# Window maxima stacked in 128 rows, zero products in TensorE's waits, and a rearranged expert tail

## The reference

```
h = rmsnorm(layernorm(x)); q, k, v = h@Wq, h@Wk, h@Wv          # 16 heads of 8
q_phi, k_phi = taylor(q@Wqf), taylor(k@Wkf)                    # 1, x, x_i*x_j
lin = causal linear attention of q_phi, k_phi, v in chunks of 128 tokens,
      with a state (kv, ksum) that is carried from chunk to chunk
win = softmax(where(allowed, q@k.T / sqrt(8), -inf)) @ v       # allowed: the last 64 tokens
x = x + layernorm(x) + concat(lin, win) @ Wout
y = layernorm(x)
topv, topi = top_k(y@Wgate + bgate, 2); topw = softmax(topv)   # 2 of 8 experts
z = (y@W1[e] + b1[e]) * (y@W2[e] + b2[e])
o = silu(z@Wg[e] + bg[e]) * (z@Wl[e] + bl[e])
out = x + sum over the 2 experts of topw * (o@W3[e] + b3[e])
```

## Time and profile before

| | |
|---|---|
| median of 3 runs | 412.84 us (408.07 to 413.14) |
| the profiled execution | 410.21 us, span 408.3 us |
| busy of the span | PE 84%, PEld 73%, DVE 62%, ACT 52%, POOL 54% |
| mean granted TensorE clock | 0.946 of full speed |
| chain that ended last | PE 73%, SPq 9%, DMA 6%, DVE 4%, ACT 2% |

### The profile page before, as it was taken

The page is one execution under the profiler, slowest core; times in us unless marked ns, Lnnn a source line. Parts: engine busy times, 40 slices in busy tenths (PEclk is TensorE's granted clock), DMA queues, the critical chain, the costliest instruction groups (busy, mean ns, idle before and its releaser), DMA issues.

```text
span 408.3 us, 15626 instructions
## 1 busy us (share of the span) xinstructions
PE 343.6 (84%) x5603; PEld 298.1 (73%) x5603; DVE 251.6 (62%) x1001; ACT 211.6 (52%) x574; POOL 219.0 (54%) x368
## 2 busy tenths in 40 slices
PE   0768795699999999999999941699999999999920
PEld 0345584588878788888888830599999999999910
DVE  4665553268986688888887747255555555555515
ACT  0465563366565766676667620355555555555410
POOL 5363554155666577767765554012666655666510
PEclk9999999699999999999999985599999999999985
DMA  7746886878887877554342000223333333333028
GB/s 197 196 123 115 141 218 149 99 166 180 182 188 177 170 134 133 135 128 92 80 92 63 18 32 28 73 60 120 118 122 125 120 127 134 114 119 119 18 67 244
DMA packets 91966, 50.20 MB, mean 123 GB/s; under 512 B 56874, under 2 KB 86220, under 8 KB 91890
## 3 DMA queue, kind: packets, MB, share of 16 engines
q1 hardware_dynamic: 88898, 44.48, 46.0%
q0 software_dynamic: 2272, 4.46, 3.4%
q10 hardware_dynamic: 720, 0.26, 0.3%
HBM read 29.52 MB, written 11.98 MB: 102 GB/s over the span
## 4 chain that ended last, share of the span: by engine, by line
PE 73%; SPq 9%; DMA 6%; DVE 4%; issue 4%; ACT 2%; POOL 1%; DVEq 0%; POOLq 0%; ACTq 0%
PE ps L748 8%; PE ps L754 8%; PE ps L642 6%; PE ps L589 5%; PE ps L720 5%; PE ps L723 4%; PE ps L731 4%; PE ps L638 4%; PE ps L688 4%; PE ps L681 4%; PE ps L601 3%; PE ps L608 3%; SPq L382 3%; SPq L368 3%; PE ps L664 2%
## 5 line engine op out<-in xcount | busy, mean ns | idle before, releaser
L1300 POOL TENSOR_SCALAR_AFFINE_SELECT amat<-amat 128x512 f32<-128x512 f32 x64 | 41.0, 641 | 66.4 <-ACT amat L820 65.7
L1334 POOL DMA_INDIRECT results<-qas,mrowid x39 | 38.2, 979 | 68.1 <-ACT qas L887 68.1
L1103 DVE TENSOR_REDUCE mrow<-ps 128x4 f32<-128x512 f32 x64 | 43.8, 685 | 36.5 <-PE ps L589 36.4
L833 ACT ACTIVATE pmat<-ps 128x512 f32<-128x512 f32 x64 | 38.4, 600 | 54.0 <-PE ps L642 54.0
L1172 DVE SCALAR_TENSOR_TENSOR qas<-ps,bcol,qas 128x128 f32<-128x128 f32 x78 | 26.5, 351 | 34.3 <-ACT qas L893 30.8
L875 ACT ACTIVATE qas<-ps,bcol 128x128 f32<-128x128 f32 x78 | 24.4, 364 | 38.4 <-PE ps L720 38.4
L1182 DVE SCALAR_TENSOR_TENSOR qas<-ps,bcol,qas 128x128 f32<-128x128 f32 x78 | 23.9, 347 | 29.0 <-ACT qas L875 21.7
L820 ACT ACTIVATE amat<-ps 128x512 f32<-128x512 f32 x64 | 38.5, 602 | 1.9 <-PE ps L601 1.7
L1261 POOL DMA_INDIRECT routed<-routed_row,slot x32 | 32.6, 1018 | 12.9 <-issue 5.8
L642 PE MATMUL ps<-minus_ident,mrow 128*128 128x128 bf16 x256 | 36.0, 221 | 0.0
L642 PE MATMUL ps<-minus_ident,mlow 128*128 128x128 bf16 x256 | 35.7, 220 | 0.0
(11 more groups left out here) (170 smaller groups left out, 913.8 us busy)
## 6 DMA issues: line engine op xcount, KB each, us to landing
kv_tok<-w SPq DMA_DIRECT2D x31, 256.0 KB
qa_parts<-wgl SPq DMA_DIRECT2D x12, 256.0 KB, 3.3
ks<-k_parts SPq DMA_DIRECT2D x32, 96.0 KB
qas<-qa_parts SPq DMA_DIRECT2D x32, 96.0 KB
xin<-routed SPq DMA_DIRECT2D x39, 72.0 KB, 1.9
ks<-k_parts SPq DMA_DIRECT2D x32, 64.0 KB
qas<-qa_parts SPq DMA_DIRECT2D x32, 64.0 KB
w<-in_W SPq DMA_DIRECT2D x2, 1024.0 KB
```

What stands on the lines that cost most here:

```text
L833: a_(pmat[:, u % 2].rearrange("p g t -> p (g t)"), ps[:, ST, :], ACT.Exp).then_inc(exp_done, 1)
L1103: v.tensor_reduce(mrow[:, b], ps[:, SQ, :].rearrange("p (a k) -> p a k", k=CH), AX.X, ALU.max).then_inc(max_done, 1)
L1300: q.affine_select(out=amat[:, u % 2], in_=amat[:, u % 2], compare_op=ALU.is_ge, fill=0.0, base=0, pattern=[[0, 4], [1, CH]], channel_multi ...
L1334: q.indirect_dma_start(results, bass.IndirectOffsetOnAxis(mrowid[:, m:m + 1], 0), yw[:, m, :], None, bounds_check=RESULTS - 1, oob_is_err= ...
```

## The change

- `mrow`'s high and low parts go into `mstack` [128, 2, 2, 4]: for the even head of a pair the high part lies in rows 0 to 63 and the low part in rows 64 to 127, for the odd head the other way round. ScalarE copies the high parts (`high_parts`, two copies, in its list right behind each exponential and for the next unit), VectorE subtracts into the low parts (two instructions in place of one). `minus_ident` is two stacked identities of 64 columns, so that one product per head, 64 columns wide, subtracts both parts.
- `window_scores` computes 32 rows by 128 columns at a time, 16 products a unit in place of 8.
- `keep_running` multiplies zeros (`still`) into a bank that is free at that point: 18 and 4 times 512 columns at the start, several times between the last steps of `post` (`BETWEEN`), 30 times 512 columns ahead of the experts and 6 times 128 after the first tile's transpose.
- In the experts ScalarE weights b3 ahead of time (`b3w`), for which it reads the tile's expert from the table, and VectorE makes `yw` in one instruction from the product, the weight and `b3w`.
- Rows of `results` are numbered so that a partition's 16 rows lie side by side; SP loads one half in four DMAs, ScalarE's queue the other.

```diff
-    vals[:, :, :, 1] = (np.arange(CH)[:, None] + CH * np.arange(NC)[None])[:, :, None] + N * np.arange(TOPK)
+    vals[:, :, :, 1] = (NC * np.arange(CH)[:, None] + np.arange(NC)[None])[:, :, None] + N * np.arange(TOPK)
-    c["minus_ident"] = (-np.eye(128, dtype=np.float32)).astype(bf)
+    c["minus_ident"] = -np.concatenate([np.eye(WINDOW, dtype=np.float32)] * 2).astype(bf)
...
+        BETWEEN = (((12, 128), (12, 128), (6, 512), (7, 512)), ((0, 0), (6, 128), (6, 512), (0, 0)))
...
@@ sync
-                for k in range(2):
-                    lo = k * N + g * GT
-                    sp.dma_start(res[k][:, g * GC:(g + 1) * GC], results[lo:lo + GT, :].rearrange("(c p) d -> p c d", p=CH)).then_inc(res_in[g], 16)
+                sp.dma_start(res[0][:, g * GC:(g + 1) * GC], half_of_results(0)[:, g * GC:(g + 1) * GC]).then_inc(res_in[g], 16)
@@ tensor
+            def keep_running(times, cols):
+                for _ in range(times):
+                    mm(ps[:, PHI, 0:cols], still[:, 0:128], still[:, 0:cols], start=True, stop=True)
...
+            pe.wait_ge(still_ready, 1)
+            keep_running(18, 512)
             pe.wait_ge(i_in, 16)
             transposes(0)
+            keep_running(4, 512)
...
-                    t = mm(ps[r:r + WINDOW, SQ, ...], qs[:, p, h, j * WINDOW:(j + 1) * WINDOW], ks[:, p, j, h, :], ...)
+                    for z in range(0, WINDOW, 32):
+                        r, at = WINDOW * (hh % 2) + z, j * WINDOW + z
+                        t = mm(ps[r:r + 32, SQ, ...], qs[:, p, h, at:at + 32], ks[:, p, j, h, :], ...)
...
                     pe.wait_ge(mlow_ready, n + 1)
+                    pe.wait_ge(mhigh_ready, n + 1)
-                    for pr in range(4):
-                        for part in (mhigh, mlow):
-                            t = mm(ps[:, ST, pr * CH:(pr + 1) * CH], part[:, u % 2, pr:pr + 1].to_broadcast([128, 128]), minus_ident[:],
+                    for hh in range(8):
+                        t = mm(ps[:, ST, hh * WINDOW:(hh + 1) * WINDOW],
+                               mstack[:, u % 2, hh % 2, hh // 2:hh // 2 + 1].to_broadcast([128, 128]), minus_ident[:],
...
                     post(c, u, c % 2)
+                    keep_running(*BETWEEN[c - NC][u])
             pe.wait_ge(r_count, NC)
+            keep_running(30, 512)
...
+                if j == -1:
+                    keep_running(6, 128)
@@ scalar
+            def high_parts(n, b):
+                act.wait_ge(max_done, n + 1)
+                if n > 1:
+                    act.wait_ge(st_ready, n - 1)
+                nc.scalar.copy(mstack[0:WINDOW, b, 0], mhigh[0:WINDOW, b])
+                nc.scalar.copy(mstack[WINDOW:, b, 1], mhigh[WINDOW:, b]).then_inc(mhigh_ready, 1)
...
                     a_(pmat[:, u % 2].rearrange("p g t -> p (g t)"), ps[:, ST, :], ACT.Exp).then_inc(exp_done, 1)
+                    if n < UNITS * NC - 1:
+                        high_parts(n + 1, (u + 1) % 2)
...
-                    a_(yw[:, m, :], yb[:, (k + 1) % 2, :], ACT.Copy, scale=mweight[:, m:m + 1]).then_inc(y_weighted, 1)
+                    a_(b3w[:, k % 2, :], b3[:, bass.ds(expert(0), 1), :]..., ACT.Copy, scale=mweight[:, k:k + 1]).then_inc(b3w_ready, 1)
...
+                act.dma_start(res[1][:, g * GC:(g + 1) * GC], half_of_results(1)[:, g * GC:(g + 1) * GC]).then_inc(res_in[g], 16)
@@ vector
+            v.memset(still[:], 0.0).then_inc(still_ready, 1)
...
-                v.tensor_tensor(mlow[:, b], mrow[:, b], mhigh[:, b], ALU.subtract).then_inc(mlow_ready, 1)
+                v.tensor_tensor(mstack[WINDOW:, b, 0], mrow[0:WINDOW, b], mhigh[0:WINDOW, b], ALU.subtract)
+                v.tensor_tensor(mstack[0:WINDOW, b, 1], mrow[WINDOW:, b], mhigh[WINDOW:, b], ALU.subtract).then_inc(mlow_ready, 1)
...
-                    v.tensor_tensor(yb[:, q, :], ps[:, Y, 0:D], flat(b3[:, bass.ds(expert(-1), 1), :]), ALU.add).then_inc(y_added, 1)
+                    v.scalar_tensor_tensor(out=yw[:, m, :], in0=ps[:, Y, 0:D], scalar=mweight[:, m:m + 1], in1=b3w[:, q, :],
+                                           op0=ALU.mult, op1=ALU.add).then_inc(y_weighted, 1)
```

More of the change, by code:

```diff
@@ L230, in build @@
         yw = late2[:, 2560:3072].rearrange("p (a d) -> p a d", a=4)
-        yb = late2[:, 3072:3328].rearrange("p (a d) -> p a d", a=2)
+        b3w = late2[:, 3072:3328].rearrange("p (a d) -> p a d", a=2)
         xin = sb("xin", [CH, 4, ROW])
@@ L237, in build @@
         ps = ctx.enter_context(nc.psum_tensor("ps", [128, 8, 512], F32))
+        still = sb("still", [128, 512], BF16)
         SQ, ST, A, OUT0, OUT1, PHI, KV, TR = range(8)
@@ L244, in build @@
         zeroed = sem("zeroed")
+        still_ready = sem("still_ready")
         wstep, wstep_c = sem("wstep"), sem("wstep_c")
@@ L329, in part_of, with half_of_results @@
             return qa[:, t // 2, part, bass.ds(g * GT, GT)]
+        def half_of_results(k):
+            return results[k * N:(k + 1) * N, :].rearrange("(p c) d -> p c d", p=CH)
         def pad_regions(engine):
@@ L587, in window_scores @@
                     h = 8 * hf + hh
-                    r = WINDOW * (hh % 2)
-                    t = mm(ps[r:r + WINDOW, SQ, (hh // 2) * CH:(hh // 2 + 1) * CH], qs[:, p, h, j * WINDOW:(j + 1) * WINDOW],
-                           ks[:, p, j, h, :], start=True, stop=True)
+                    for z in range(0, WINDOW, 32):
+                        r, at = WINDOW * (hh % 2) + z, j * WINDOW + z
+                        t = mm(ps[r:r + 32, SQ, (hh // 2) * CH:(hh // 2 + 1) * CH], qs[:, p, h, at:at + 32], ks[:, p, j, h, :],
+                               start=True, stop=True)
                 t.then_inc(sq_ready, 1)
@@ L639, in chunk @@
                            start=(hh == 0), stop=False, skip_group_check=True)
-                    for pr in range(4):
-                        for part in (mhigh, mlow):
-                            t = mm(ps[:, ST, pr * CH:(pr + 1) * CH], part[:, u % 2, pr:pr + 1].to_broadcast([128, 128]), minus_ident[:],
-                                   start=False, stop=part is mlow, skip_group_check=True)
+                    for hh in range(8):
+                        t = mm(ps[:, ST, hh * WINDOW:(hh + 1) * WINDOW],
+                               mstack[:, u % 2, hh % 2, hh // 2:hh // 2 + 1].to_broadcast([128, 128]), minus_ident[:],
+                               start=False, stop=True, skip_group_check=True)
                     t.then_inc(st_ready, 1)
@@ L728, in step @@
                     if j > 1:
[L729 removed]
+                        pe.wait_ge(y_weighted, j - 1)
                     for h in range(2):
@@ L855, in _ @@
             act.wait_ge(xaffine, 1)
+            high_parts(0, 0)
             squares(0, 0)
@@ L880, in step @@
                     nc.scalar.copy(xT[:, k % 2, :], ps[:, TX, 0:CH]).then_inc(xT_copied, 1)
[L881 to L885, removed]
-                        act.wait_ge(y_out[m], 16 * turn(-1))
-                    a_(yw[:, m, :], yb[:, (k + 1) % 2, :], ACT.Copy, scale=mweight[:, m:m + 1]).then_inc(y_weighted, 1)
-                if on(0):
+                if on(0):
+                    act.wait_ge(meta_copied, j + 1)
+                    if j >= 2:
+                        act.wait_ge(y_weighted, j - 1)
+                    a_(b3w[:, k % 2, :], b3[:, bass.ds(expert(0), 1), :].rearrange("p a f -> p (a f)"), ACT.Copy,
+                       scale=mweight[:, k:k + 1]).then_inc(b3w_ready, 1)
                     if j > 1:
@@ L893, in step @@
                         a_(sg[:, k % 2, h, :], ps[:, G[h], 0:CH], ACT.Silu, bias=bcol[:, k, 4 + h:5 + h]).then_inc(silu_done, 1)
-            run_steps(act, step)
+            run_steps(act, step, (0,))
+            for k in range(4):
+                act.wait_ge(y_out[k], 16 * ((NT - k + 3) // 4))
+            for g in range(NG):
+                act.dma_start(res[1][:, g * GC:(g + 1) * GC], half_of_results(1)[:, g * GC:(g + 1) * GC]).then_inc(res_in[g], 16)
         @block.vector
```

18 lines of the change are left out of this document (10 added, 8 removed).

## The result

The changed kernel takes **416.65 us** (median of 20 runs, 414.19 to 421.35) against 410.62 for the kernel before beside it (20 runs, 407.12 to 417.45): ratio 1.0144, 95% interval 1.0116 to 1.0173. It is slower, by 1.4%: clear of the noise, though less than the 2% that the prediction wanted for telling a change from none. The prediction said 405, 396 to 412.

The account below looks back on a forecast made before the run. It took TensorE as attention's bound, beside a loop of equal length (11.36 us a chunk) through VectorE and ScalarE. Attention +1.1, start -1.7, gap -0.9, first experts -2.0, end -1.6 sum to -5.1; 410.2 becomes 405, range 396 to 412.

Parts of the forecast that it names:

- the sum of the attention: Attention stage: full chunks 0.38 us longer (+3.4), chunk 7 +0.4, light chunks -2.7; in sum +1.1 us.
- the loop: Full attention chunk: reduction, copies, state copy, squares, output copies, TensorE's transposes, VectorE's stretch; 11.36 us before, 11.74 predicted.
- the rival that TensorE's saving counts: Attention: the loop does not close, period about 10.7 us, -8.6 in place of +1.1, total 395; chance 0.17.
- The subtractions, 0.09 each: VectorE's second small subtraction per unit, priced at half of 0.173 us for overlap; two in the loop, 2 x 0.09.
- The copies, 0.10 each: ScalarE's two copies of 64 x 4 per unit, assumed to overlap; 2 x 0.10 us added to the loop.
- The bound of -3 for cheap copies: Attention's lower bound: -3 us in sum if copies take 0.05 and the extra subtraction nothing.
- The rival of dear copies: Attention: each copy holds ScalarE 0.35 us, +8.8 in place of +1.1, total 413; chance 0.10.
- Subtraction of the maxima: TensorE in attention: eight 64-column products take 0.24 us instead of 0.44; 0.20 a unit, 0.8 a chunk saved.
- Window scores: TensorE in attention: 16 products onto 32 rows priced like L688, 0.33 us, no gain; bounds 0.1 either way.
- Start, gap, first experts: Zeros raise the clock: start -1.7, gap before experts -0.9, first experts -2.0 us, capped by the load of tile 4.
- Experts: Expert stage: no matmul added or removed; ScalarE's table reads in 31 steps hidden in waits for TensorE; 0.
- End: Last loads and sums: ScalarE's step leaves the last chain, -0.4; DMA issues on two queues, -1.2; together -1.6 us.

Follow-up runs that it names:

- e9: The kernel before with the zeros alone (start, between the last posts, gap, first expert step); 404.5 us, ratio 0.9888.
- e5: The changed kernel with the attention as before (old subtraction, 8 window scores of 64 rows); zeros, experts' bias step and end stay; 403.9 us, ratio 0.9817.
- e6: The kernel of e5 with results in the old order of rows (last loads in rows of 512 B), still on two queues; 403.35 us, ratio 0.9820.
- e7: The kernel of e5 with the stack for units 1 and 2 of each chunk only; 403.5 us, ratio 0.9809.
- e14: The kernel of e5 with 24 zeros at the start instead of 18; 404.0 us, ratio 0.9850.
- e15: The kernel of e7 with 24 zeros at the start; 403.3 us, ratio 0.9816.
- e1: The changed kernel with the old subtraction of the maxima, no stack; 32-row window scores, zeros, experts and end stay; 406.6 us, ratio 0.9886.
- e8: The changed kernel without ScalarE's two copies, high parts left out of the exponents; two subtractions and 64-column products stay; 407.05 us, ratio 0.9900.
- e11: The kernel of e5 with the last sums shared: GpSimd adds the residual of the first two groups, VectorE makes six sums; 405.8 us, ratio 0.9890.
- e13: The kernel of e1 with 24 zeros of 512 columns at the start instead of 18; 406.6 us, ratio 0.9890.
- e4: The changed kernel with ScalarE's list reordered: the two copies behind the state copies, output copies ahead of the squares; 411.6 us, ratio 0.9975.

## Why the prediction was wrong

**The step that failed** is the stack, in the sum of the attention: "Its length is 11.36 + 2 x 0.10 for the copies + 2 x 0.09 for the extra subtractions that lie in VectorE's stretch = 11.74." The mechanism was right: the loop closes on the way that the prediction walked, TensorE's saving is waited out in front of the transposes, and the rival that TensorE's saving counts did not come. Both terms of the sum were too small, the second the most: +0.42 and +0.67 were measured where I had +0.20 and +0.18, so a full chunk got 1.10 longer and not 0.38.

- **The subtractions, 0.09 each.** They measure 0.28 each. I took half a subtraction for the new one, since two that do not need each other overlap. In the trace before they do: behind `mlow` the next step starts after 0.08 of its 0.17 us. These two do not: the second starts 0.17 behind the first, and the next step 0.19 behind the second. So the new one costs its full length, and the overlap of the old one with the next step is lost as well. The 0.11 of VectorE's other instructions I had not counted at all.
- **The copies, 0.10 each.** They measure 0.21 from start to start: copies of 64 x 4 do not overlap with each other or with the state copy behind them. The Trainium skill (ScalarE: Activation LUTs, What ACT_TABLE_LOAD costs) gave the fixed time well, 186 ns against 190. The overlap of 93 ns from which my estimate of 0.1 came shows here behind a chunk's first exponential (186.67, 0.58 long, the copy 0.48 behind its start). It does not show between the copies, nor behind other exponentials (183.35 to 183.97 is 0.62); what decides, no run shows. The trace before had no such copy, and L851 and L852, whose 0.14 I took it from, did not stand for it.

The bound of -3 for cheap copies was also wrong in itself: by the prediction's own terms it is about -2. The light chunks gave little: the last two stretches between denominators lasted 11.41 and 9.85, against 11.37 and 10.06 before. The rival of dear copies had the right sign and came nearest (413) by a wrong price: it put 0.35 on each copy, which took 0.21; the rest was VectorE's. Its chance of 0.10 was too small for a loop whose slack I had just put at nothing.

**Subtraction of the maxima:** right, eight products in 0.24 us, and worthless. **Window scores:** 16 products take 0.34, as I gave them; pauses I had not thought of may add up to 3 us. **Start, gap, first experts:** right within 0.4 each, and the cap was the one named, SP's load of tile 4 (273.17 + 1.85, taken up by TensorE at 275.06). In e9 and e5 the start was worth more, since SP's chain shortened more than its first piece moved. **Experts:** most steps take 3.24 us as before, and ScalarE's table reads show in none of these; a few longer ones (up to 3.56) make the stretch from tile 4's transpose to the last one 0.43 longer. **End:** ScalarE's 0.4 came (from the last transpose to the last result 9.98 in place of 10.45), and those longer steps took it back; the 1.2 for the second queue did not, because I counted issue time and not the order of landings. The Trainium skill (DMA: Bandwidth & Descriptors, Specifications) says 512 B is enough for the line rate; the totals of e6 and e5, 403.35 and 403.85, agree, with no gain from rows of 2 KB.

The rest of the distance, from 414.27 to the median 416.65, lies between executions; no trace here shows what makes it.

**The fastest versions:** e5, e6, e7, e9, e14 and e15, 403.3 to 404.5, 1.1 to 1.9% below the kernel before. They keep the zeros and leave the stack out, or use it where its copies stand off the loop. e1, e8, e11 and e13, 405.8 to 407.05, beat both kernels too.

## What to carry to other kernels

A busy engine at 99% says little about a saving on it while another chain of the same length runs beside it: walk that chain through a whole period, and price every new instruction on it at its full start-to-start time, with the overlap that its neighbours lose, unless a row shows that very overlap. Copies of 0.2 us that wait for another engine, put ahead of copies that a third engine needs, made most of a loss of 10 us here, because the wait also made a longer stretch of VectorE count; half of them, off that way, cost nothing. Where zeros hold a clock, look at the pause that is left behind the last of them, in the execution where they end soonest.

## What the hardware showed that I had not expected

- Copies of 64 x 4 on ScalarE cost 0.21 us each, start to start (206.21 to 206.63 for two), more than the output copy of 128 x 128 behind which the next one starts after 0.14 to 0.15.
- VectorE's two subtractions that do not need each other start 0.17 us apart, their own length; nothing of them overlaps, and the next step starts 0.19 behind the second. Behind the one subtraction of before it started after 0.08.
- TensorE paused in the middle of groups, up to 3.5 us at a time (e13), 8.0 us in one execution between 75 and 240 (e4), 0.6 in another (before); in the one pause looked at (e1, 146.27) SP's queue alone took 101% of the DMA engines' time. I take the pauses for a source of the 6 us or so between executions of one kernel; no run shows that.
